# PNA pass of a four-layer graph network: 11 of 782 gathered chunks fetched row by row by SyncE

## What is computed

```python
m = concatenate([h[dst], h[src]], -1) @ W_pre + b_pre
mean    = segment_sum(m, dst, n) / deg
mean_sq = segment_sum(m * m, dst, n) / deg
mn = where(has, segment_min(m, dst, n), 0)
mx = where(has, segment_max(m, dst, n), 0)
std = sqrt(relu(mean_sq - mean * mean) + eps)
```

## Time and profile before

| what | value |
|---|---|
| median of 3 runs | 4626.91 us |
| lowest, highest | 4619.5, 4628.82 us |
| profiled execution, its own time | 4617.97 us |
| its span in the trace | 4615.9 us |
| PNA pass in it, first to last gather issued by POOL | 2275.5 to 3250.6 us |
| last stores of the pass | 3274.6 us |
| mean granted TensorE clock, whole span | 0.72 of full speed |

### The profile page before, as it was taken

How to read it: one execution, slowest core, us unless ns; L and a number is a source line. 1 busy time by engine, 2 the same in 40 slices (tenths; PEclk the granted TensorE clock), 3 DMA queues, 4 the chain that set the end, 5 groups by cost and what they waited for, 6 DMA issues and landing times. The chain is left out here.

```text
span 4615.9 us, 79158 instructions
## 1 busy us (share of the span) xinstructions
PE 3159.7 (68%) x19497; PEld 2667.1 (58%) x19497; DVE 3209.7 (70%) x7496; ACT 2334.3 (51%) x4887; POOL 3221.9 (70%) x3428
## 2 busy tenths in 40 slices
PE   4888888887633334334566666666696888888886
PEld 3666666665533333334455555555465777777776
DVE  5888888888633333334689898989656766667667
ACT  4766666665300000000677777777436666666665
POOL 4777777776577777777677777777315777777774
PEclk7555555555765666655788888888897888888887
DMA  7333333332122222221388888888623333333332
GB/s 140 89 89 86 88 87 89 87 88 61 48 55 55 56 56 55 56 57 51 114 291 290 286 290 289 296 283 295 200 76 87 83 80 82 80 80 82 82 80 76
DMA packets 368300, 567.20 MB, mean 123 GB/s; under 512 B 107029, under 2 KB 171192, under 8 KB 367861
## 3 DMA queue, kind: packets, MB, share of 16 engines
q1 hardware_dynamic: 254190, 332.06, 22.5%
q0 software_dynamic: 106720, 227.64, 20.2%
q10 hardware_dynamic: 6950, 2.44, 0.2%
HBM read 328.98 MB, written 230.89 MB: 121 GB/s over the span
## 5 line engine op out<-in xcount | busy, mean ns | idle before, releaser
L896 POOL DMA_INDIRECT e_G<-dr_tab,src_idx x830 | 792.7, 955 | 272.4 <-issue 233.5
L896 POOL DMA_INDIRECT v_G<-dr_tab,src_idx x830 | 790.3, 952 | 253.3 <-issue 247.4
L2123 POOL DMA_INDIRECT m_G<-dr_tab,chunk_src x782 | 738.0, 944 | 247.1 <-issue 238.0
L1899 POOL DMA_INDIRECT s_G<-dr_tab,chunk_src x760 | 717.5, 944 | 235.6 <-issue 226.5
L2007 PE MATMUL s_OUT<-s_G,s_S 128*128 x1664 | 375.3, 416 | 560.5 <-POOLq L1892 525.3
L2007 PEld LDWEIGHTS s_OUT<-s_G,s_S 128*128 128x128 f32 x1664 | 349.9, 320 | 585.6 <-issue 585.6
L1953 DVE TENSOR_TENSOR ACC<-ACC,s_OUT 128x129 f32 x832 | 241.3, 290 | 592.1 <-PE s_OUT L2007 475.7
L2269 PE MATMUL m_BK<-eye,m_XT 128*128 128x128 f32 x3136 | 492.5, 310 | 155.1 <-ACT m_XB L2182 149.8
L2182 ACT COPY m_XB<-m_BK 128x512 f32<-128x512 f32 x784 | 428.0, 592 | 276.1 <-PE m_BK L2269 275.1
L2269 PEld LDWEIGHTS m_BK<-eye,m_XT 128*128 128x128 f32 x3136 | 408.3, 161 | 230.5 <-issue 187.6
L1329 PE MATMUL e_OUT<-e_RH,e_S 128*128 128x144 f32 x1664 | 511.9, 476 | 1.9 <-DVE e_RH L1215 1.9
(11 more groups left out here) (377 smaller groups left out, 7207.7 us busy)
## 6 DMA issues: line engine op xcount, KB each, us to landing
dr_ends<-m_XB SPq DMA_DIRECT2D x392, 512.0 KB, 3.9
e_LR<-dr_row_loc SPq DMA_DIRECT2D x104, 256.0 KB
v_LR<-dr_row_loc SPq DMA_DIRECT2D x104, 256.0 KB
m_SAME<-dr_row_same SPq DMA_DIRECT2D x98, 256.0 KB, 6.5
s_G<-dr_tab SPq DMA_DIRECT2D x1408, 0.5 KB
s_G<-dr_tab ACTq DMA_DIRECT2D x1408, 0.5 KB
e_G<-dr_tab,src_idx POOLq DMA_INDIRECT x830
v_G<-dr_tab,src_idx POOLq DMA_INDIRECT x830
```

The source lines that it names most:

```text
L896: pool.indirect_dma_start(out=out, out_offset=None, in_=table, in_offset=bass.IndirectOffsetOnAxis(ap=g["src_idx"][:, step:step + 1], axis ...
L1899: pool.indirect_dma_start(out=G[:, c % (RING * GROUP), 0:D], out_offset=None, in_=table[:, :], in_offset=bass.IndirectOffsetOnAxis(ap=g["c ...
L2123: pool.indirect_dma_start(out=G[:, k % Q, c % GROUP, :], out_offset=None, in_=table[:, :], in_offset=bass.IndirectOffsetOnAxis(ap=g["chunk ...
```

## The change

SP fetches the last chunk of the groups 10, 18, ..., 90 (11 chunks) row by row, and POOL leaves them out. The rows of one chunk are spread over eight groups of SP's program, 16 rows in each (chunk n over the groups 8n to 8n+7), and chunk n is used by PE in group 8n+10. In each of the 88 groups SP reads 16 byte offsets into registers by one TENSOR_LOAD, then issues four row DMAs before the first store, and four before each of the other three. The rows go to two buffers of their own, `GX`, which lie with the index row in a part of the tensor `XR3n` that this pass leaves free. At the start SP loads the source numbers of the 11 chunks (11 DMAs of 512 bytes), and DVE turns them into byte offsets by one shift over 1408 numbers on one partition, for which SP waits. The table is seen as bytes, so the register is the address offset without arithmetic on SP.

```diff
+PIECE = 16
+PNA_FETCHED = [k * GROUP + GROUP - 1 for k in range(10, PICKS - 2, P // PIECE)]
...
+def load_places(nc, places, row):
+
+    _, vals = nc.values_load_multi_w_load_instructions(
+        places, engines=[mybir.EngineType.SP], min_val=0, max_val=(N - 1) * row,
+        skip_runtime_bounds_check_because="the sources are numbers of nodes, here times the bytes of a row")
+    return vals
...
+        lo = PARTS * D
+        GX = fin.spare[:, lo:lo + 2 * D].rearrange("p (b d) -> p b d", b=2)
+        INDEX = fin.spare[0:1, lo + 2 * D:lo + 2 * D + len(PNA_FETCHED) * P].bitcast(I32).rearrange("o (n e) -> o n e", e=P)
+        table_bytes = table.bitcast(U8).rearrange("(o r) b -> o (r b)", o=1)
...
+        def gathers(k):
+            return [c for c in range(k * GROUP, min((k + 1) * GROUP, CHUNKS)) if c not in PNA_FETCHED]
...
                 for k in range(PICKS):
                     wait(pool, gt_done, k - Q + 1)
-                    for c in range(k * GROUP, min((k + 1) * GROUP, CHUNKS)):
+                    for c in gathers(k):
                         pool.indirect_dma_start(out=G[:, k % Q, c % GROUP, :], out_offset=None, in_=table[:, :],
...
+                for n, c in enumerate(PNA_FETCHED):
+                    sp.dma_start(INDEX[:, n, :], src[c * P:(c + 1) * P].unsqueeze(0)).then_inc(index_in, 16)
                 for k in range(4):
                     same(k)
                 sp.wait_ge(start, 4)
                 sp.dma_start(rows[:, 0, :], zero).then_inc(zero_stored, 16)
+                sp.wait_ge(index_bytes, 1)
                 for k in range(PICKS):
                     if 1 <= k and k + 3 < PICKS:
                         sp.wait_ge(scanned, PARTS * k)
                         same(k + 3)
+                    n, p = k // (P // PIECE), k % (P // PIECE) * PIECE
+                    places = load_places(nc, INDEX[:, n, p:p + PIECE], 4 * D) if n < len(PNA_FETCHED) else []
+                    if places and p == 0:
+                        wait(sp, gt_done, PNA_FETCHED[n - 2] // GROUP + 1 if n >= 2 else 0)
+
+                    def fetch(some):
+                        for u in some:
+                            if places:
+                                sp.dma_start(GX[p + u:p + u + 1, n % 2, :].bitcast(U8),
+                                             table_bytes[:, bass.ds(places[u], 4 * D)]).then_inc(fetched[n % 2], 16)
+                    fetch(range(0, 4))
                     for q in range(PAIRS):
+                        if q:
+                            fetch(range(4 * q, 4 * q + 4))
                         sp.wait_ge(xb_done, halves(k, PARTS - 1) + q // 2 + 1)
...
+                dve.wait_ge(index_in, 16 * len(PNA_FETCHED))
+                V.tensor_single_scalar(INDEX, INDEX, 9, op=ALU.logical_shift_left).then_inc(index_bytes, 1)
...
+                    rows, n = rows_of(k)
+                    if n is not None:
+                        pe.wait_ge(fetched[n % 2], 16 * P * (n // 2 + 1))
                     for s in range(GROUP):
-                        ins = nc.tensor.transpose(GT[:, k % 2, s * P:(s + 1) * P], G[:, k % Q, s, :], g["eye"][:])
+                        row = GX[:, n % 2, :] if n is not None and s == GROUP - 1 else rows[:, s, :]
+                        ins = nc.tensor.transpose(GT[:, k % 2, s * P:(s + 1) * P], row, g["eye"][:])
```

More of the change, by code:

```diff
@@ L13 @@
 import math
-F32, I32, BF16 = mybir.dt.float32, mybir.dt.int32, mybir.dt.bfloat16
+F32, I32, BF16, U8 = mybir.dt.float32, mybir.dt.int32, mybir.dt.bfloat16, mybir.dt.uint8
 ALU, ACT, AX = mybir.AluOpType, mybir.ActivationFunctionType, mybir.AxisListType
@@ L2051, in factors_of_counts, with moments_pass @@
         dve.wait_ge(chain, 3)
-def moments_pass(nc, g, table, extremes, fin):
+def moments_pass(nc, g, table, extremes, fin, src):
     name = "m_"
@@ L2099, in moments_pass @@
         base = g["rows_gathered"][:]
+        index_in = sem("index_in")
+        index_bytes = sem("index_bytes")
+        fetched = [sem(f"fetched{b}") for b in range(2)]
         same_in = [sem(f"same_in{b}") for b in range(4)]
@@ L2109, in moments_pass, with rows_of @@
         xb_done = sem("xb_done")
+        def gathers(k):
+            return [c for c in range(k * GROUP, min((k + 1) * GROUP, CHUNKS)) if c not in PNA_FETCHED]
         def landings(k):
-            return 16 * (min((k + 1) * GROUP, CHUNKS) - k * GROUP + k // Q * GROUP)
+            return 16 * sum(len(gathers(j)) for j in range(k % Q, k + 1, Q))
+        def rows_of(k):
+            return G[:, k % Q], (PNA_FETCHED.index(k * GROUP + GROUP - 1) if k * GROUP + GROUP - 1 in PNA_FETCHED else None)
         def halves(k, i):
@@ L2810, in layer_gcn, with layer_pna @@
         gcn_to_pna(nc, g, ACC)
-def layer_pna(nc, g, XR):
+def layer_pna(nc, g, XR, src):
     with ExitStack() as ctx:
         fin = PnaFinish(nc, g, ctx, XR)
-        moments_pass(nc, g, g["tab2"], g["ends2"], fin)
+        moments_pass(nc, g, g["tab2"], g["ends2"], fin, src)
         pna_to_gatv2(nc, g, XR, fin)
@@ L2876, in gnn_kernel @@
         with nc.sbuf_tensor("XR3n", [P, TILES, D], F32) as XR:
-            layer_pna(nc, g, XR)
+            layer_pna(nc, g, XR, w["src"])
             layer_gatv2(nc, g, XR, out)
```

## The result

Against the kernel before, timed beside it (4626.66 us), the changed kernel takes 4700.62 us: ratio 1.016, 95% interval 1.0149 to 1.0171. It is 74 us **slower**, where 13.7 us of gain were forecast. The profiled execution took 4693.14 us, with a span of 4691.0. So the sign was wrong. Of the rivals only one has this sign, SP as the bound, and what follows looks for it.

The account below looks back on a forecast made before the run. POOL was taken to set the pace, at 9.99 us a group. Leaving out 11 gathers was to give -13.7 us and everything else nothing: 4613.2 us against the median of 4626.91, range 4604 to 4632 us.

Parts of the forecast that it names:

- Point 1: On POOL: leaving out 11 gathers of 1.2485 us makes its last gather 13.7 us earlier, all on the path.
- Point 2: On SP's queue: rows, load, stores and flags take 8.7 us a group, under 9.83, so the new work costs nothing.
- The load: SP's TENSOR_LOAD of 16 offsets in each group: 1.0 us, bounds 0.78 and 1.56.
- The rows: SP's 16 row DMAs in each group: 0.35 us a row, 5.5 us.
- Stores and flags: SP's four stores and the flags in each group: 5 x 0.45 = 2.2 us.
- that wait passes behind the rows: On SP's queue: 1.4 us of row fetches between two stores hide the later store's wait for the 512 KB before it.
- Rival B: SP's queue becomes the bound from 9.83 us a group: 4654 us at 10.3, 4874 us at 12.8; chance 12%.
- Points 3 and 4: Stores start up to 3.6 us later for ACT, SP's rows land about when PE wants them: nothing, bound 11 us for rows.
- rival D: SP's rows or stores come late for PE or ACT: 11 us back, 4624 us; chance 8%.
- Point 5: On the DMA engines: bytes stay, 16 rows make 0.6 us a group, nothing when spread over 16 engines.
- Point 6: At the pass's start: SP's 11 loads take 3.2 us, hidden with DVE's shift in ACT's and DVE's idle time; nothing.
- Rival C: The chain behind POOL (PE, DVE, ACT) takes the pace and half of the gain stays: 4620 us; chance 16%.

Follow-up runs that it names:

- skip_fetch: Changed kernel with POOL still leaving out the 11 gathers, but SP fetching nothing (no TENSOR_LOAD, no row DMA): 4614.46 us, ratio 0.997.
- one_load: Changed kernel with all 1408 row DMAs, but a single TENSOR_LOAD in the first group whose offsets serve for all: 4614.26 us, ratio 0.997.
- load_only: Changed kernel without row DMAs, meant to keep one TENSOR_LOAD a group, but its trace holds none: 4612.31 us, ratio 0.9965.
- load_quiet: Changed kernel with one row in the first four a group, and the load moved behind SP's wait for ACT's copies: 4605.28 us.
- late16: Changed kernel with four rows behind each store, then the load of the next group's offsets, then the flags: 4662.79 us, ratio 1.0084.
- rows12: Changed kernel with 12 rows a group, each chunk over 11 groups, 8 chunks off POOL: 4611.53 us, ratio 0.9979.
- late12: Changed kernel with the 12 rows a group of rows12 in the order of late16: 4612.09 us, ratio 0.9979.
- all_gathers: Changed kernel with SP's new work whole, but POOL gathering all 782 chunks again: 4702.94 us, ratio 1.0165.
- two_stores: Changed kernel with two stores of 1 MB a group for four of 512 KB, eight rows ahead of each: 4753.31 us, ratio 1.0295.

## Why the prediction was wrong

**Point 1, POOL's 11 gathers: right.** 13.7 us forecast, 12.7 and 12.9 measured where SP kept up (skip_fetch, one_load), 14.8 in load_only, which is skip_fetch's program.

**Point 2, SP's sum: the step that failed.** It forecast 8.7 us a group, with 8.4 and 12.8 as bounds, and the group took 10.95. Term by term:

- *The load*: 1.0 us with bounds of 0.78 and 1.56; it took 2.07 in the mean. This is the larger of the two errors, by little, and lies outside its bounds. I priced it by its count alone, from a row of the GCN pass in which no large transfer stood ahead of it in the queue. In a quiet queue it would have been right (1.15 in load_quiet).
- *The rows*: 5.5 us (16 x 0.35 is 5.6); 16 rows of 0.304 and 0.10 between them are 6.5. A row that isn't held has 0.33 us from start to start, as the 0.35 wanted, but of the four behind a store the third is held, and takes 0.54 us and not 0.23. So "that wait passes behind the rows" was wrong: the queue's wait didn't vanish, it went over from the next store to a row. The argument stood in the rival's part ("a row DMA behind a store might wait just so") and was given no price in the sum.
- *Stores and flags*: 2.2 us; about 1.9 for the stores and 0.55 for the flags.

Together 11.0 us against 10.95 measured. Without the load's error the group would have been about 9.9, at the very edge: late16 at 10.59, with longer rows, says that the load's place isn't enough by itself. It takes both errors to get the 1.1 us over POOL's pace, and only a kernel with less of one of them (one_load, rows12) is back under it.

**Rival B: what happened**, by its own signs: SP without waits, groups over 9.9 us apart, and POOL's gaps ending by a free buffer. The runs bracket its point of decision, 9.83 us a group: where SP still has waits (rows12, late12) nothing is lost, and 10.59 us in late16 costs 41 us; no run lies nearer. (That 0.42 us a row reaches this point is a slip: with the rest of point 2 it gives 9.9, over it.) Its price, (10.95 - 9.99) x 88 = 84 us, is 10 over the 74 measured. 4654 us was worked out for 10.3; 12% was too little for a term with bounds from 8.4 to 12.8 and its edge at 9.83. Two thirds of that interval lay beyond the edge.

**Points 3 and 4, stores and rows in time: wrong in the profile, but as a consequence.** ACT's 138.0 us and PE's 41.2 us of waiting are there because SP is late. In one_load, with every row DMA in place, these waits are 0 and 4.1 us and all of the gain is there, so rival D had no cost of its own.

**Point 5, DMA engines: right.** one_load shows it, with 1408 row DMAs and all of the gain. The Trainium skill's rule that a transfer which isn't split runs on the lowest engine (DMA: Bandwidth & Descriptors, "Why a DMA increments its semaphore by 16 and not by 1") stays unseen here, since the trace doesn't tell the engines apart.

The other rule that was weighed, under point 2, says that a transfer's start costs its sequencer usually little beside the transfer (the Trainium skill, DMA: Bandwidth & Descriptors, "Issuing engines are not separate DMA queues"); by it the forecast would have stayed as it was. What the trace set against it was 0.42 us of SP for each such row; here it is 0.40, and the runs side with the trace.

**Point 6, the start: right.** The timeline there, to be read with the earlier trace rows:

```profile
2276.92 3.24 SPq L2166 DMA_DIRECT2D XR3n<-in_src_dram  x11
...
2281.40 0.88 DVE L2271 TENSOR_SCALAR XR3n<-XR3n 1x1408 int32<-1x1408 int32 x1 [5.08 <-DMA XR3n<-in_src_dram]
...
2283.85 1.15 ACT L2205 ACTIVATE m_UP<-m_SAME,m_big 128x1024 bf16<-128x1024 bf16 x1 [13.89 <-DMA m_SAME<-dr_row_same]
...
2290.31 0.26 DVE L2259 COPY m_sums_f<-m_BK 128x98 f32<-128x98 f32 x1 [6.88 <-PE m_BK L2322]
```

The loads took 3.24 us (3.2 forecast), ACT began at 2283.85 (2283.3), and DVE still waits 6.88 us for PE, though its copy comes 0.9 us later than before. POOL's first gather starts 0.4 us later than before.

**Rival C, the chain: not seen as a cause.** In skip_fetch, one_load and rows12 POOL runs through without a wait for a buffer, and the last copy is done 20.4, 22.6 and 21.4 us after the last gather's start. In the changed kernel it is 41 us (3306.3 to 3347.3), far over the 25 us that were named as C's sign; but so it is in every run in which SP is late (40 to 41 us in all_gathers, two_stores and late16), and in none in which SP keeps up. So this sign doesn't tell C from B. With SP in front the granted clock of the stretch fell from 0.85 to 0.78, nearer to the lower of its two levels, 1.2 GHz: PE does fewer matmuls there (3215 against 3493 in the same 870 us) and is busy for 64% of it, before for 62%. That is a consequence too; in one_load and rows12 the clock is 0.87 and 0.86.

What stays open is how earlier transfers lengthen a TENSOR_LOAD. It doesn't wait for them to land: in the changed kernel the flags just ahead of it (L2163) need at least 4.3 us from issue to landing, by the 24 of 98 whose landing the trace tells, and the load ends 2.6 us after their issue in the median, 3.0 at most.

```profile
DMA to landing us min/median/max: 4.3/4.8/6.4
```

Whether it waits for an earlier stage of them, or is only slowed, the runs don't say. Nor does any run put the large transfers on another engine's queue, so that it must be SP's own queue is argued, not shown.

## What to carry to other kernels

An engine's queue that only issues DMAs is a resource with a sum of its own: add up what it holds for one turn of the loop, with what stands ahead of each instruction *in this loop*, before giving it work "in its waiting time". SP waited for 604 of 975 us and had 5.5 us a group free between the flags and the next store. Work forecast at 4.2 us a group took 6.4, and so 12 rows a group won 10 us where 16 lost 74. And where a term's bounds reach far across the point at which the sign turns, the other sign deserves more than a corner of the chances.

## What the runs showed of the hardware

- A TENSOR_LOAD on SP takes longer when large transfers of its own queue have just been issued. With 16 numbers, medians: 1.15 us with nothing large in the last 3 us, 1.23 behind four row DMAs and 1.7 us after a store, 2.08 behind a store of 512 KB and flags of 256, 3.15 behind four such stores in a burst and flags, 3.27 behind one of 1 MB and flags. With 8 numbers: 0.78 behind row DMAs, 1.88 us behind a store of 512 KB and flags.
- SP's queue needs about 1.2 us for a 512 KB store once it is filled, while the issue of one alone shows 0.39 us. In the changed kernel's timeline the first group without rows has all its copies ready, and its four stores stand back to back, right behind a store and flags; the next group's four come 4 us after the flags:

```profile
3267.07 3.96 SPq L2191 DMA_DIRECT2D dr_ends<-m_XB  x4
...
3276.28 3.06 SPq L2191 DMA_DIRECT2D dr_ends<-m_XB  x4
```

  The first four make (3.96 - 0.39) / 3 = 1.2 us for each after the first; of the second four only the third and the fourth are held (0.36, 0.47, 0.85 and 1.25 us). Of small DMAs behind one such store two pass almost without a hold-up and the third is held; behind 1 MB the third and the fourth are held, about 1.0 and 0.8 us. The wait shows at a DMA issued soon after, so other DMAs of the same queue, put there, don't hide it.
- A load into registers that nothing uses isn't in the program that runs, which load_only shows (no TENSOR_LOAD in its trace); such a probe needs a use for its result.
